# One layer stack on one core: key stacks fetched in three transfers, a reordered stage boundary, and biases moved to VectorE

## What is computed

```python
x = x + _L0_xattn_ref(_layernorm(x), ctx, ctx, mask, Wq, bq, Wk, bk, Wv, bv, Wo, bo)  # 16 heads of 16 dims, 4096 keys
x = x + _L0_attn_ref(_layernorm(x), ...)   # rmsnorm, in-projection, gate, two depthwise convolutions, fuse, out
x = x + _L0_ffn_ref(_layernorm(x), ...)    # quantised feed-forward, gelu
x = x + _L1_xattn_ref(_layernorm(x), ctx, ctx, mask_ff, Wq, bq, Wk, bk, Wv, bv)        # one head
x = x + _L1_attn_ref(_layernorm(x), ...)   # 8 causal and 8 full heads with rotary embedding
x = x + _L1_ffn_ref(_layernorm(x), ...)    # 8 experts, 2 chosen per token, capacity 64
return x
```

```python
vals, idx = jax.lax.top_k(dot2, K)
masked = jnp.full_like(dot2, -jnp.inf).at[rows, idx].set(vals)
weights = jax.nn.softmax(masked, axis=-1)
ones = (weights > 0).astype(weights.dtype)
cap_ones = jnp.where(jnp.cumsum(ones, axis=0) <= expert_capacity, ones, 0.0)
```

## Time and profile before

| | us |
|---|---|
| time, median of 3 runs | 946.79 |
| lowest and highest | 945.58 and 948.34 |
| the profiled execution's own time | 946.52 |
| its span, first to last instruction | 944.6 |
| PE busy in the span | 892.6 (94%) |
| DVE busy | 609.9 (65%) |
| ACT busy | 471.9 (50%) |
| POOL busy | 108.9 (12%) |

### The profile page before, as it was taken

One profiled execution on the slowest core, in us unless ns is written; L12 is line 12 of the kernel. 1 busy time (PEld: TensorE's weight loads), 2 busy tenths in 40 slices (PEclk: granted clock), 3 DMA queues, 4 the chain that ended last, 5 costly groups with the idle time before them and its releaser, 6 DMA issues.

```text
span 944.6 us, 15469 instructions
## 1 busy us (share of the span) xinstructions
PE 892.6 (94%) x6067; PEld 529.1 (56%) x6067; DVE 609.9 (65%) x1089; ACT 471.9 (50%) x946; POOL 108.9 (12%) x127
## 2 busy tenths in 40 slices
PE   6799799999999999999999998999999999988998
PEld 3356344444546665455545586754874874555745
DVE  5889477777886556888854386877624227369452
ACT  3241466777776566777779542214411310567211
POOL 2330011111000000000000200010100006245200
PEclk9999899999999999999999899999999999999999
DMA  9975633544323112222603800084546550000000
GB/s 301 295 222 173 206 106 117 151 130 140 107 68 107 41 34 68 68 68 68 215 2 129 298 31 1 1 275 148 200 178 252 193 163 16 1 1 1 1 0 23
DMA packets 68884, 108.68 MB, mean 115 GB/s; under 512 B 7110, under 2 KB 42950, under 8 KB 66886
## 3 DMA queue, kind: packets, MB, share of 16 engines
q1 hardware_dynamic: 65516, 100.61, 33.5%
q10 hardware_dynamic: 3296, 7.08, 2.3%
HBM read 93.77 MB, written 13.89 MB: 114 GB/s over the span
## 4 chain that ended last, share of the span: by engine, by line
PE 81%; DVE 7%; ACT 5%; DMA 3%; issue 2%; POOL 1%; SPq 0%; ACTq 0%; DVEq 0%
PE psum L1912 13%; PE psum L1894 11%; PE psum L1859 11%; PE psum L2292 6%; PE psum L2320 5%; PE psum L1836 5%; PE psum L2429 4%; PE psum L2053 4%; PE psum L1826 4%; PE psum L2066 3%; ACT arena L790 2%; PE psum L2483 2%; PE psum L2468 1%; PE psum L2501 1%; DVE arena L1185 1%
## 5 line engine op out<-in xcount | busy, mean ns | idle before, releaser
L1185 DVE TENSOR_REDUCE arena<-psum 128x1 f32<-128x1024 f32 x256 | 301.1, 1219 | 107.1 <-PE psum L1859 106.6
L790 ACT ACTIVATE arena<-psum 128x512 f32<-128x512 f32 x512 | 263.6, 604 | 68.0 <-PE psum L1894 66.8
L1859 PE MATMUL psum<-arena 96*128 96x512 bf16 x512 | 153.0, 381 | 9.8 <-DMA arena<-kparts 4.6
L1894 PE MATMUL psum<-arena 99*128 99x256 bf16 x1024 | 155.1, 274 | 3.5 <-ACT arena L781 1.2
L1912 PE MATMUL psum<-arena 128*32 128x256 f32 x2048 | 137.3, 386 | 0.1
L1894 PEld LDWEIGHTS psum<-arena 99*128 99x128 bf16 x1024 | 80.6, 97 | 98.2 <-ACT arena L790 36.7
L1912 PEld LDWEIGHTS psum<-arena 128*32 128x32 f32 x2048 | 53.5, 109 | 75.5 <-ACT arena L790 31.1
L1826 PE MATMUL psum<-arena 128*128 128x512 f32 x128 | 63.8, 626 | 10.7 <-DMA arena<-ctxT 9.5
L1859 PEld LDWEIGHTS psum<-arena 96*128 96x128 bf16 x512 | 48.9, 98 | 28.9 <-DVE arena L1185 11.4
L664 POOL TENSOR_TENSOR arena<-arena 128x512 bf16<-128x512 f32 x34 | 41.4, 1217 | 194.7 <-DVE arena L1171 192.1
L1836 PE MATMUL psum<-arena 128*128 128x256 f32 x256 | 63.4, 384 | 0.0
(11 more groups left out here) (258 smaller groups left out, 965.9 us busy)
## 6 DMA issues: line engine op xcount, KB each, us to landing
arena<-kparts SPq DMA_DIRECT2D x192, 128.0 KB, 3.1
kparts<-arena SPq DMA_DIRECT2D x32, 384.0 KB, 3.3
arena<-ctxT SPq DMA_DIRECT2D x20, 512.0 KB, 5.9
arena<-mask SPq DMA_DIRECT2D x8, 1024.0 KB, 5.1
arena<-ctx SPq DMA_DIRECT2D x2, 4096.0 KB, 16.8
arena<-mask ACTq DMA_DIRECT2D x4, 1024.0 KB, 13.7
arena<-ctxT SPq DMA_DIRECT2D x1, 4096.0 KB, 14.0
arena<-ctxT SPq DMA_DIRECT2D x4, 1024.0 KB, 8.1
```

The lines of the kernel that those rows point to most:

```text
L790: nc.scalar.activation(PR[step % 4][:, pair * CH:(pair + 1) * CH], exp_bank(step, pair), ACT.Exp)\
L1185: nc.vector.tensor_reduce(MX[g % 2][:, col:col + 1], unit_banks(n).rearrange("p b n -> p (b n)"), AX.X, ALU.max).then_inc(s_maxed, 1)
L1859: last = nc.tensor.matmul(out, q, KST[g % 2][0:ROWS, j, at], start=True, stop=not masked, skip_group_check=True)
L1894: last = nc.tensor.matmul(heads[:, u, :], KST[gg % 2][0:KROWS, j, kc * P:(kc + 1) * P], QST[0:KROWS, G * g + j, b * S:(b + 1) * S], start= ...
```

## The change

It has five parts.

1. *Layout and stacks.* Head dims come ahead of heads in the key and query projections (the weights' rows are permuted outside of the kernel), so that the four heads of a group are contiguous in DRAM. Rows of products are grouped by key part: partitions 0 to 47 take key part 0, 48 to 79 part 1, 80 to 95 part 2. A quarter of a stack comes in three transfers of 48, 32 and 16 rows of 8 KB; the first two read the same 16 rows of DRAM three times and twice, by a source whose first dimension has count 3 or 2 and step zero. The query stack has three transfers too, with no repeated source; the query store is one.
2. *Ones by memset*, by POOL: one early, one after the last key piece of sequence 0. The six loads of ctx of sequence 1 move from the end of SP's start list to ACT's list, one behind each value copy.
3. *Loop end by sequence.* The context of sequence 0 is turned inside of the last loop pass, the projection by `WO`, the norm and its turn go by sequence, DVE adds `bo` to X ahead of time, the second norm's result is added after the gates, and the square root's table is asked for early. `convolve_a` moves ahead of `project_hb(0)` and of `fuse`.
4. *Row biases by VectorE* for `out_b` and the second attention's `BV`, in place of `bias_rows`.
5. *Experts chosen first.* DVE reads the logits from PSUM, makes `CHOSENB` from one comparison of the exponential with 0, and makes the shares after `SEL`; `keep_awake` has 14 matmuls for 20.

```diff
-K_PARTS = (0, 0, 0, 1, 1, 2)
-Q_PARTS = (0, 1, 2, 0, 1, 0)
+K_ROWS = ((0, 3), (3, 5), (5, 6))
-        KST = [b16(8192 * i, 16384).rearrange("p (j n) -> p j n", j=G) for i in range(2)]
+        KST = [b16(8192 * i, 16384).rearrange("p (c j n) -> p c j n", c=QUARTERS, j=G) for i in range(2)]
-        kparts = nc.dram_tensor("kparts", [B, 3, D, S2], BF16, kind="Internal").ap()
+        kparts = nc.dram_tensor("kparts", [B, QUARTERS, 3, D, 2 * CH], BF16, kind="Internal").ap()
...
-            sp.dma_start(arena[ROWS:KROWS, 0:8192], t["ones"]).then_inc(q_stacked, 16)
...
             def load_stack(gg, quarter):
                 b, g = gg // GPB, gg % GPB
-                for r in range(6):
-                    src = kparts[b, K_PARTS[r], g * G * DH:(g + 1) * G * DH, at]
-                    sp.dma_start(KST[gg % 2][r:ROWS:6, :, at],
-                                 src.rearrange("(j d) n -> d j n", d=DH)).then_inc(k_stacked[gg % 2][quarter], 16)
+                for part, (first, last) in enumerate(K_ROWS):
+                    src = kparts[b, quarter, part].rearrange("(d h) n -> d (h n)", d=DH)[:, g * G * 2 * CH:(g + 1) * G * 2 * CH]
+                    sp.dma_start(KST[gg % 2][first * DH:last * DH, quarter].rearrange("p j n -> p (j n)"),
+                                 src.unsqueeze(0).broadcast_to((last - first, DH, G * 2 * CH)))\
+                      .then_inc(k_stacked[gg % 2][quarter], 16)
...
-            for c in range(SLOTS):
-                first_values_done(c + 2)
-                load_ctx(1, c, 0)
...
+            def ones_for_maxima(i):
+                nc.gpsimd.memset(arena[ROWS:KROWS, 8192 * i:8192 * (i + 1)], TWO_ONES).then_inc(built, 1)
+                pool.wait_ge(built, 9 + i)
+            pool.wait_ge(built, 8)
+            ones_for_maxima(0)
...
-                for row in range(6):
-                    act.dma_start(QST[row:ROWS:6, :, 0:S],
-                                  qparts[Q_PARTS[row], :, 0:S].rearrange("(h d) n -> d h n", d=DH)).then_inc(q_stacked, 16)
+                for first, last in K_ROWS:
+                    act.dma_start(QST[first * DH:last * DH, 0].rearrange("p h n -> p (h n)"),
+                                  qparts[0, 0:last - first].rearrange("r (d h) n -> (r d) (h n)", d=DH))\
+                       .then_inc(q_stacked, 16)
+            def load_next_ctx(c):
+                act.wait_ge(ring_drained, VALUE_AT[0, c + 2, 1] + 1)
+                n = load_number(1, c, 0)
+                act.dma_start(CTX[n % SLOTS], ctx_chunk(1, c)).then_inc(ctx_loaded[n % SLOTS], 16)
...
+            dve.wait_ge(on["rows_loaded"], 48)
+            add_rows(row("bo"))
+            add_attention(0)
+            attention_stats(0)
+            normalise(NG - 1)
+            add_attention(1)
+            attention_stats(1)
+            normalise_for_mix(0)
+            add_attention(2)
+            attention_stats(2)
+            add_attention(3)
+            attention_stats(3)
+            normalise_for_mix(1)
...
             for m in range(IT):
                 gate(0, m)
+            add_normalised()
             silu(1, 1)
...
+            add_rows(row("out_b"))
             add_mixed(0, 1, TT)
...
             dve.wait_ge(on["g_logits"], 3)
-            mark(nc.vector.tensor_scalar(den, egap, 1.0, None, ALU.add))
+            mark(nc.vector.scalar_tensor_tensor(out=pick, in0=over_e(egap), scalar=0.0, in1=hot2,
+                                                op0=ALU.is_gt, op1=ALU.mult))
             done()
+            nc.vector.tensor_tensor(CHOSENB, hot1, pick, ALU.add).then_inc(on["g_chosen"], 1)
...
+                        if gg + 1 == GROUPS and m == KC // 2 - 1:
+                            pe.wait_ge(on["w_quantised"], 1)
+                            pe.wait_ge(norm_step, 3 * GPB)
+                            turn_rows(CTXN, 0, SUM_BANK)
...
-                bias_rows([psum[:, i, 0:256] for i in range(TT)], row("bo")[0:1, :])
-                pe.wait_ge(norm_step, 3 * NG)
-                turn(CTXN, 0)
                 turned()
-                for i in range(TT):
-                    linear_rows(psum[:, i, 0:256], tok(HTC, i), WO, True, "b_out")
+                attention_out(0)
+                turn_context(GROUPS - 1)
+                attention_out(1)
                 pe.wait_ge(on["mix_loaded"], 80)
                 pe.wait_ge(on["bm_loaded"], 48)
+                pe.wait_ge(norm_step, 3 * NG)
+                turn_rows(CTXN, 1, 7)
...
+                attention_out(2)
+                for i in range(2):
+                    pe.wait_ge(h_ready, TT + i + 1)
+                turn_rows(HS, 0, 7)
+                attention_out(3)
...
+                pe.wait_ge(on["c_a_weights"], 4 + IT * TAPS_A)
+                convolve_a(0)
                 pe.wait_ge(on["c_in_copied"], 16)
                 pe.wait_ge(on["c_hbpw_copied"], IT + 2)
                 project_hb(0)
-                convolve_a(0)
                 project_ha(0)
+                convolve_a(1)
...
-            keep_awake(6, 20)
+            keep_awake(6, 14)
```

243 lines of the change are left out of this document (141 added, 102 removed).

## The result

The changed kernel takes 965.71 us (median of 4 runs, 965.12 to 968.46) for 946.44 of the kernel before beside it: a ratio of 1.021, 95% interval 1.0193 to 1.0226. The forecast was 950.2 with a range of 924 to 959. The direction was right, and so was the mechanism (few engines carry the key stacks); the loss is +19.3 us where +3.4 was forecast. The profiled execution is the longest of the four (968.46, span 966.3), so differences of spans, 21.7 us in all, are 2.4 more than those of the medians.

A forecast was written before the change was run, and what follows sets the result against it. PE, busy for 94% of the span, was taken to bound the kernel; +22.0 - 6.0 - 10.7 + 0.5 - 1.3 - 1.1 = +3.4 on 946.52 gave 949.9, or 950.2 as median, range 924 to 959.

The forecast's parts named there:

- The few engines: Stack loads: a transfer is shared among as many of 16 engines as its first dimension divides into, so 3, 2 and 16.
- the rival of the sixteen engines: Stack loads: quarters spread over sixteen engines after all, 1.9 us each; about 923, or 928 with a smaller mix gain; chance 0.27.
- The price: Start, stack loads on few engines: PE 20.1 us late at units 24 to 31, plus 1.9 of slow clock, +22.0 us.
- The engine that is in all three needs 10.4 us for a quarter: Stack loads: the busiest engine moves its packets at 26 GB/s; sixteen engines would need 1.9 us.
- my chain: Start: from first issue at 34.2, quarters, query stack, 12 stores, ctx chunks and gaps put the fourth quarter at 105.3 us.
- the few engines bind the main loop too: Main loop: at 13.6 us a quarter against 11.5, the last 8 to 16 quarters delay PE; near 973, 0.05 including memset.
- Ctx: First main loop pass: ACT issues ctx chunks, so PE's stall of 3.93, slow clock of 1.9 and 0.2 go: -6.0 us.
- Ones by memset: Start, POOL: contiguous memset ends at 11.4, cost 0; at the strided price it ends at 19.0, 3 us on the start.
- Loop end and mix: Loop's end to quantising: PE's in-projections finish 9.7 us earlier, quantising -10.7; PE's later wait may cost clock, +0.5.
- Row biases of the second attention: Second attention: biases of 1.99 us leave PE, 0.6 becomes a wait for DVE's last normalised tile: -1.3 us.
- Experts: Expert choice: one copy of 0.23 leaves the chain and six small instructions of 1.17 become one of 0.22: -1.1 us.
- the slower quarters: Main loop bound by stack quarters at 13.6 us each, near 973; chance 0.05 together with a memset delaying the start.

The follow-up runs named there:

- distinct_rows: Changed kernel with the repeated rows replaced by different key parts, whose rows lie in even steps: 927.95 us, ratio 0.9813 to the kernel before.
- padded_rows: As distinct_rows, with 16 unused rows behind each key part in DRAM so the steps are uneven: 967.52 us, ratio 1.022.
- changed_moved: Changed kernel with the three copies placed on partitions 32 to 79 and the two on 0 to 31: 960.35 us, ratio 1.0143.
- pair_held: Changed kernel with three copies as plain transfers, SP also waiting for stack 0's fourth quarter before issuing stack 1: 944.91 us, ratio 0.9979.
- triple_only: Changed kernel with the part of two copies as two plain transfers, the three copies still one transfer: 950.73 us, ratio 1.0048.
- dim_first: Changed kernel with the 16 head dims as the source's first dimension and the copies second, partitions to match: 928.32 us, ratio 0.9814.
- ctx_late: dim_first with sequence 1's six ctx chunks issued by SP at its start list's end, not by ACT: 932.6 us, ratio 0.9847.
- mix_alone: Kernel before with only the change's third part, plus out_b's rows added by VectorE: 936.87 us, ratio 0.9901.
- triple_moved: triple_only with the three copies placed on partitions 32 to 79 and the two on 0 to 31: 947.29 us, ratio 1.0013.
- six_plain: Changed kernel with each stack quarter fetched by six plain transfers of 16 rows, no repeated source: 930.49 us, ratio 0.9838.
- early_moved: dim_first with ACT's query stack loads issued earlier and the three copies placed on partitions 32 to 79: 923.17 us, ratio 0.9754.

## Why the prediction was wrong

**The few engines: right as a mechanism.** "I take it that a transfer is shared among as many of the 16 engines as its first dimension divides into" stood on three packets of `ones` and held, with the first dimension taken after even steps are joined (distinct_rows against padded_rows); the rival of the sixteen engines was wrong for this kernel and right, at 928, for the one with the dimensions turned.

**The price is the step that failed:** the term "layout and stacks", +22.0, was mis-sized. By the table it is 31.3 + 2.4 + 6.4 (the 7.0 less the turn of 0.6 that moved into the loop) = +40.1. The 18.1 us of difference are - 3.7 (the first issue came earlier than the 34.2 I began with) + 7.5 + 7.4 (both below, as they stand at unit 24) + 0.5 of clock + 6.4. Four things are in them.

*Two engines through one port.* "The engine that is in all three needs 10.4 us for a quarter": a lone quarter took 14.3. The share-out (3, 2 and 16) and the engine's 26 GB/s were both right, as changed_moved shows with 11.2 us; that the first and third copy write partitions 32 apart was not thought of. It is worth 7.4 us at unit 24 (116.47 to 109.09) and 5 to 6 us of time (965.7 to 960.3; by the ratios, 1.021 to 1.0143, 6.3).

*Company.* With 10.4 us a quarter my chain ends at 105.3 for units 24. It began at 34.2, the first issue of before; changed_moved issues at 30.5, which makes it 101.6. Its units begin at 109.09, 7.5 later:

```profile
109.09 1.86 PE L1925 MATMUL psum<-arena 96*128 96x512 bf16 x4 [9.72 <-DMA arena<-kparts]
```

Between 4 and 5 us of it are there at the first unit, which begins at 49.22, where "the first lands near 48", moved by the same 3.7, is 44 to 45. In the start packets of stores, ctx and queries run on the same engines, and I had given each its own bytes at 26 or 20 GB/s and nothing more. In changed_moved the 8 KB packets from 32 to 40 us take 0.56 us in the mean, for 0.31 late in a lone quarter. pair_held shows that such company is costly: its late quarter came 8.1 us sooner once the others were quiet. That company is all of these 4 to 5 us is argued and not tested.

*A miscount.* Between the first unit and unit 24 the chain has about 57 us and changed_moved 59.9. The sum counts "12 stores between the quarters" and "one ctx chunk in SP's list". The list has 13 stores and two chunks before `load_stack(0, 3)`: 2.8 us more by the forecast's own prices, and that is about the rest of the 7.5.

*What stands behind in SP's list.* I had argued that stack 1 lands ahead of the loop's need, and it does: no unit in the loop waits for `kparts`. I didn't ask which stores are queued behind it. SP came to them 30 us late, and PE waited 4.22 us at 172.42 for ACT and then ran slow; 6.4 in all. changed_moved has a wait of 3.9 us at that place too; dim_first has none.

That triple_only came out at 950.73, next to the forecast's 950.2, is chance: its quarter of 11.0 us is near the forecast's, its SP list is not.

The rival "the few engines bind the main loop too" named 13.6 us and 11.5 as the least time of a loop quarter. Lone quarters took 14.3, and still no unit in the loop waited; nine quarters behind each other, from 392.5 to 503.6 us, took 12.3 each.

**Ctx:** -6.0 forecast, -5.0 measured in the trace, -3 to -4 in ctx_late. The first key projection of the loop, at 138.46, has no wait, and its four matmuls take 1.88 us for 3.78. "No wait for ctx in either case" was too strong: at 74.58 PE waits 1.30 us for a late chunk of sequence 0 from SP's list, ahead of a longer wait for the stack.

**Ones by memset:** no cost, as forecast.

```profile
3.06 6.92 POOL L659 MEMSET arena<- 3x8192 f32 x1
15.57 1.55 POOL L667 TENSOR_TENSOR arena<-arena 128x512 bf16<-128x512 f32 x1 [5.59 <-DVE arena L1204]
```

The memset ends at 9.98 (11.4 forecast), 0.84 ns an element: the contiguous one of the two rows.

**Loop end and mix:** forecast -10.7, and +0.5 for the clock. In-projections begin 8.0 us behind the loop's end (8.4 among the forecast's signs, 7.7 by its own sum, 16.6 before). Until they end it is 29.4 us for 39.15, -9.7 as forecast. DVE's timeline, for the earlier trace rows:

```profile
609.68 1.90 DVE L1448 SCALAR_TENSOR_TENSOR arena<-psum,arena 128x256 f32<-128x256 f32 x4
...
614.92 1.42 DVE L1400 TENSOR_TENSOR arena<-arena 128x256 f32<-128x256 f32 x4
...
618.78 0.47 DVE L1495 SCALAR_TENSOR_TENSOR arena<-arena 128x256 f32<-128x256 f32 x1
```

Gates 45.4 us behind the loop's end (45.6 forecast), quantising 54.5 (55.1). PE then waits 3.03 us (2.8 forecast), and the eight products behind it take 3.08 for 1.94: the clock's window:

```profile
621.90:625.30 3.40, 3.18 (x11) 2.38 (x13) 2.41 (x9) 0.38 (x1) 0.00 (x0) 0.60 0.00 0
```

That is +1.1, inside its 0 to 1.9. The stage gives -10.2, or -9.6 with the turn in the loop, for a forecast of -10.2; mix_alone has -9.4.

**Row biases of the second attention:** -2.7 for -1.3. The projection behind them takes 3.72 us for 5.41: it runs at full clock (1.00 in that stretch, 0.62 before), which I hadn't seen. That it is the one-row matmuls ahead of it that had cost the clock is not shown; more than they changed there. **Experts:** -1.1 to the count (-1.1 forecast).

```profile
928.40 0.19 DVE L1834 SCALAR_TENSOR_TENSOR arena<-arena 128x32 f32<-128x32 f32 x1 [0.27 <-ACT arena L1133]
928.62 0.19 DVE L1837 TENSOR_TENSOR arena<-arena 128x32 bf16<-128x32 f32 x1
```

From the exponential to `CHOSENB` it is 0.22 us, for 1.17.

**The range** failed with the price: the slower quarters had 0.05 together with the memset, and it ended at 959.

Open: how much of the 4 to 5 us of company comes from which transfer; how much the ports explain of the 192 to 211 GB/s of all sixteen engines; and why the profiled execution is 2.75 us longer than the median.

## What to carry to other kernels

Put a dimension with a multiple of 16 outermost in both sides of a transfer, and copies behind it: here that alone is worth 37 us of 966, with the same bytes and the same number of transfers. Before transfers are merged or made slower, read the issuing engine's list to its end: issues can block (12.6 us for one here), and what they delay may be a store that another engine waits for; here it came 30 us late. When one transfer stops being the last to arrive, look at the next: once the key stack was in time, the query stack held the first unit for 5.2 us, and two moved lines gave 4 us.

## What was not expected of the hardware

Three engines that write partitions 0 to 15, 16 to 31 and 32 to 47 in step moved 57 GB/s (triple_only), on 32 to 79 they moved 76 (triple_moved): in the packet records one of 8 KB takes 0.31 us alone and 0.6 where two engines meet. Sixteen engines with all parts of a quarter moved 145 GB/s in six transfers on 16 neighbouring partitions each (six_plain), 197 in three (dim_first) and 211 with the placing altered (early_moved; 192 before it), where loads of the start had 3.13 MB in 8 us, 391 GB/s. An issue of a stack transfer on SP took up to 12.6 us in the changed kernel's start, for 0.67 in the median. A memset of 8192 elements on 3 partitions took 6.92 us on POOL.
